# Gated cross-attention with a routed feed-forward: where ScalarE rounds the expert weights, and in which order GpSimd serves roots and low parts

## The chip, the cores and the metric

The kernel runs on one core of one Trainium2 chip. The metric is the device time of one execution in microseconds (us), lower is better; the median of three runs is compared.

## The reference

Eight batches of 256 rows of 512 numbers. First an attention over a context, added to the rows with a gate; then a layer normalisation, a router that picks two of eight experts for each row, and the two experts' feed-forward, again added with a gate. All is float32.

```python
x = x + tanh(g_xattn[0]) * xattn(layernorm(x), ctx_2048, mask)
x = x + tanh(g_ffn[0]) * ffn(layernorm(x), w_router, w_gate, w_up, w_down)
# xattn: softmax(mask(h @ ctx.T / sqrt(512))) @ ctx
# ffn: probs = softmax(h @ w_router.T); top 2, rescaled to sum 1
#      sum over the two experts of p * (silu(h @ Wg.T) * (h @ Wu.T)) @ Wd.T
```

## The kernel before

It has two stages. The first, some 125 us long, walks over 16 tiles of 128 rows (NTK = 16, two tiles to a batch): attention, second normalisation, router, and a table that sorts the rows by expert. The second gathers the sorted rows and runs the experts over 36 to 39 tiles. The change touches the first stage only.

The first stage is a software pipeline written out by hand. Each of the five engines runs its own program, a loop `for s in range(STEPS)`, and works in step s on several tiles at once, each at another place of its way. Semaphores join the programs; within one engine the order is as written, so an instruction that waits holds back all that stand behind it.

What matters of a step s:

- TensorE (PE): `t1(s)` transposes the normalised tile (L914), `tp(s-2)` transposes the softmax numerators (L920), `score(s-1)` (L932), the router product `rt(s-4)` (L962), the attention product `pv(s-2)` (L943), `t2(s-3)` transposes the second normalised tile (L951), and in odd steps the small products `cum` and `tab` of the sorting table (L974 to L986). From step 16 on `pv` stands ahead of `rt`.
- ScalarE (ACT): copies out of PSUM `ev2(s-4)` (L486) and `ev1(s)` (L463), the first normalisation `xln(s+1)` (L493), two stores, `evp(s-2)` (L479), in odd steps a small exponential (L524), then the second normalisation `x2ln(s-3)` (L501), the softmax exponential `exp(s-1)` (L470), and last the roundings `hi(u)` (L506) of the step's weight blocks.
- VectorE (DVE): a main list, with one operation of a side list woven in after each of its operations. Main: `X` update of tile s-3 (L652), its statistics (L611, L614, L617), the statistics of tile s+2 (the same lines), the bias `nb2(s-3)` (L626), the row maximum (L632), the bias `nb1(s+2)` (L626 again), the reciprocal (L644). Side: router top 2 and sorting, such as `dd` (L672), `MS` (L681), `Qi` (L703), `rr` (L706), `TA` (L711), four `TB` (L718), and `cc`, `pc`, `comb` (L730 to L737). In even steps the side list runs from the top 2 to two of the `TB`; in odd steps from the other two to `comb`.
- GpSimd (POOL): the two roots of a step, `rstd` of tile s-3 (`rs2`) and of tile s+2 (`rs1`), both at L370, and the low parts `lo(u)` at L379.

The expert weights come in 40 blocks of 128x512. ScalarE writes the rounded value of a block (`hi`, which signals `s_wh`), and GpSimd then writes the difference between the block and its rounding (`lo`, which waits for that signal). `units(s)` names the blocks of a step: one in steps 1 and 2, two in steps 3 to 17, one in steps 18 to 21; the other four are done in the second stage. SyncE loads the blocks of step s+2 during its own step s.

VectorE has to have `rs2` for `nb2`, and `x2ln(s-3)` needs `nb2`; PE's `t2(s-3)`, the last large product of its step, needs `x2ln(s-3)`.

Of the kernel before, what the change touches and what calls it, by code (L numbers as in the profile page):

```python
# [8 lines left out]
NTK = 16  # L9
# [12 lines left out]
NXT = 7  # L22
EPS = 1e-5
RB = 6
AHEAD = 12

SCALE = float(D) ** -0.5
# [2 lines left out]
def flamingo(nc, x, ctxn, ctxt, mask, gates, wr, wgu, wd1, wd2, cst, cstb, out):  # L30
# [11 lines left out]
    with ctx:  # L42
# [209 lines left out]
        def part(u):  # L252

            return u // 5, (u % 5 if u < NU - 5 else (u - 1) % 5)

        def wunit(u):

            e, n = part(u)
            if n < 3:
                c = slice(1536 * e + 512 * n, 1536 * e + 512 * n + 512)  # L260
                return wgu[3 * e + n], WGlf[:, c].bitcast(fp32), WGhf[:, c], WGlf[:, c]
            if n == 4:
                return wd2[e], WS[:, e % 2, :], WD2[:, e, :], WD2[64:128, e, :]
            return wd1[e], WD1l[:, e, :].bitcast(fp32), WD1h[:, e, :], WD1l[:, e, :]

        def units(s):

            return range(*[min(NUA, sum(SPLIT[:max(0, n)])) for n in (s, s + 1)])
# [6 lines left out]
        def tiles_of(eng):  # L275

            eng.wait_ge(s_ln, 1)
            return eng.value_load(LN[0:1, 0:1], min_val=NF, max_val=NT)

        def lives(eng, n, j):  # L280

            return eng.If(n > j) if j >= NF else nullcontext()
# [73 lines left out]
        @block.gpsimd  # L356
        def _(pool):
            pool.wait_ge(s_c, 16)

            last = [None]  # L360

            def settle():

                if last[0]:
                    pool.wait_ge(*last[0])

            def rstd(mv, k, rs, s_in, s_out):
                last[0] = (s_out, k + 1)
                pool.wait_ge(s_in, k + 1)
                pool.tensor_tensor(out=rs[:, k:k + 1], in0=mv[:, k, 1:2], in1=mhalf, op=ALU.pow).then_inc(s_out, 1)  # L370

            def lo(u):
                pool.wait_ge(s_wh, u + 1)
                _, raw, hi, low = wunit(u)
                half = part(u)[1] == 4
                p = slice(64, 128) if half else slice(0, 128)
                if half:
                    settle()
                pool.tensor_tensor(out=low, in0=raw[p], in1=hi[p].bitcast(fp32), op=ALU.subtract).then_inc(s_wl, 1)  # L379
                last[0] = (s_wl, u + 1)  # L380
                if half:
                    settle()

            rstd(mv1, 0, rs1, s_st1, s_rs1)
            rstd(mv1, 1, rs1, s_st1, s_rs1)
            for s in range(STEPS):
                if s != NTK + 2:
                    for u in units(s - 1)[0:1]:
                        lo(u)
                if 0 <= s - 3 < NTK:  # L390
                    rstd(mv2, s - 3, rs2, s_st2, s_rs2)
                for u in units(s - 1)[0 if s == NTK + 2 else 1:]:
                    lo(u)
                if s + 2 < NTK:
                    rstd(mv1, s + 2, rs1, s_st1, s_rs1)


            pool.wait_ge(s_ixg, 1)
            pool.wait_ge(s_sy[0], 16 * 8)
            pool.wait_ge(s_sy[1], 16 * 8)  # L400
            pool.wait_ge(s_scb, 16 * 8)
            for i in range(4):
                pool.wait_ge(s_so[i], 16 * 4)

            def gather(j):
                if j >= NX:
                    pool.wait_ge(s_tx, j - NX + 1)
                    pool.wait_ge(s_cj, j - NX + 1)
                pool.indirect_dma_start(out=XG[:, j % NX, :], out_offset=None, in_=x2s,  # L409
                                        in_offset=bass.IndirectOffsetOnAxis(ap=IXG[:, j:j + 1], axis=0))\  # L410
                    .then_inc(s_g[j % NX], 16)

            def landed(n):

                for i in range(NB):
                    if (n + NB - 1 - i) // NB:
                        pool.wait_ge(s_add[i], 16 * ((n + NB - 1 - i) // NB))

            def fence(j):

                with pool.If((turns[(j - 1) // 13] & (1 << (j - 1) % 13)) != 0):
                    landed(j)

            for j in range(NX):
                gather(j)
            pool.wait_ge(s_tn, 1)
            pool.wait_ge(s_ixi, 1)
            turns = [pool.value_load(TN[0:1, g:g + 1], min_val=0, max_val=(1 << 13) - 1) for g in range(3)]
            live = tiles_of(pool)
            for j in range(NT):  # L430
                with lives(pool, live, j):
                    pool.wait_ge(s_y, j + 1)
                    if j:
                        fence(j)
                    pool.indirect_dma_start(out=out, out_offset=bass.IndirectOffsetOnAxis(ap=IXI[:, j:j + 1], axis=0),  # L435
                                            in_=YT[:, j % NB, :], in_offset=None, compute_op=ALU.add)\
                        .then_inc(s_add[j % NB], 16)
                    if j + NX < NT:
                        gather(j + NX)
                    if j in HOLD:  # L440
                        lo(NUA + HOLD.index(j))
# [3 lines left out]
        def _(act):  # L445
# [36 lines left out]
            def ev2(k):  # L482
                act.wait_ge(s_t2, k + 1)
                if k >= 1:
                    act.wait_ge(s_rt, k)
                act.activation(Y2T[:, :, :], A1[:, :].rearrange("p (k c) -> p k c", k=KC), ACT.Copy)\  # L486
                    .then_inc(s_y2t, 1)
# [16 lines left out]
            def hi(u):  # L504
                act.wait_ge(s_ws[u % NST], 16 * (u // NST + 1))
                act.activation(wunit(u)[2], wunit(u)[1], ACT.Copy).then_inc(s_wh, 1)  # L506

            xln(0)
            for s in range(STEPS):
                if 0 <= s - 4 < NTK:  # L510
                    ev2(s - 4)
                if s < NTK:
                    ev1(s)
                if s + 1 < NTK:
                    xln(s + 1)
                stores(s)
                if 0 <= s - 2 < NTK:
                    evp(s - 2)
                if s >= 7 and s % 2 == 1 and (s - 7) // 2 < B:
                    b = (s - 7) // 2  # L520
                    act.wait_ge(s_dd, b + 1)
                    if b:
                        act.wait_ge(s_cb, b)
                    act.activation(e2[:, :, :], dd[:, :, :], ACT.Exp).then_inc(s_e2, 1)  # L524
                if 0 <= s - 3 < NTK:
                    x2ln(s - 3)
                if 0 <= s - 1 < NTK:
                    exp(s - 1)
                for u in units(s):
                    hi(u)  # L530

            act.activation(rsum[:, 0:1], rinv[:, 0:1], ACT.Silu)
            act.wait_ge(s_ejp, 1)
# [12 lines left out]
            def silu(j):  # L546
                act.wait_ge(s_gu, j + 1)
                if j >= 2:
                    act.wait_ge(s_h, j - 1)
                act.activation(SG[:, j % 2, :], SC[j % 2][:, 0:I], ACT.Silu).then_inc(s_sg, 1)  # L550
# [18 lines left out]
            for j in range(NT):  # L569
                with lives(act, live, j):  # L570
                    silu(j)
                    if j == AHEAD:
                        live = tiles_of(act)
# [13 lines left out]
        def _(dve):  # L587
# [87 lines left out]
            def ranks(b):  # L675
# [6 lines left out]
                yield  # L682
                if b >= RB:
                    return
# [205 lines left out]
            for j in range(NT):  # L890
                with lives(dve, live, j):
                    mul(j)
                    if j == AHEAD:
                        live = tiles_of(dve)
# [8 lines left out]
        def _(pe):  # L903
# [61 lines left out]
            def cum(b):  # L965
# [3 lines left out]
                else:  # L969
                    pe.wait_ge(s_gbc, 1)  # L970
                pe.wait_ge(s_rn, min(b, RB) + 1)
                for i in range(2):
                    o = PC[:, 8 * i:8 * i + 8]
                    pe.matmul(o, tri, MS[:, b, i, :], start=True, stop=False)  # L974
                    pe.matmul(o, onesb, ebr, start=False, stop=False)
                    for t in range(2 * RB, 2 * b) if b > RB else ():
                        pe.matmul(o, onesb, MS[:, t // 2, t % 2, :], start=False, stop=False)
                    if i:
                        pe.matmul(o, onesb, MS[:, b, 0, :], start=False, stop=False)
                    m = pe.matmul(o, onesb, Rn[:, min(b, RB), :], start=False, stop=True)  # L980
                m.then_inc(s_cum, 1)
# [11 lines left out]
            for s in range(STEPS):  # L993
# [32 lines left out]
                if s == 2 * B + 5:  # L1026
                    pe.wait_ge(s_ms, B)
                    pe.wait_ge(s_lc, B - 1)
                    for t in range(2 * RB, 2 * B):
                        pe.matmul(PL[:, 0:8], onesb, MS[:, t // 2, t % 2, :], start=(t == 2 * RB), stop=False)  # L1030
                    pe.matmul(PL[:, 0:8], onesb, Rn[:, RB, :], start=False, stop=True).then_inc(s_cnt, 1)
# [71 lines left out]
            for j in range(NT):  # L1103
                with lives(pe, live, j):
# [6 lines left out]
                    if j % 2 == 1 and 2 * j + 2 < NTP:  # L1111
                        own.update(experts(2 * j + 2))
                    if j == AHEAD + NT - NF:
                        live = tiles_of(pe)
# [69 lines left out]
```

## Time and profile before

| | |
|---|---|
| median of 3 runs | 290.98 us (290.82 to 292.32) |
| the profiled execution | 291.58 us, of it 289.8 us span |
| PE busy | 255.7 us, 88% of the span |
| DVE busy | 168.7 us, 58% |
| POOL busy | 164.1 us, 57% |
| ACT busy | 148.7 us, 51% |
| mean granted TensorE clock | 0.94 |

The profile is one execution of the program. A timeline row gives the start in us from the span's beginning, the duration, the engine, the line of the kernel, the operation with what it writes and reads, how many instructions the row merges, and in brackets how long the engine was idle before it and who released it. A duration that is longer than that of the same operation elsewhere holds time in which the instruction had begun and couldn't go on.

The first stage has three parts: the filling of the pipeline to about 40 us, the steady pairs of steps (an even and an odd one) to about 95 us, and the tail to about 126 us, where only the last tiles and the sorting table are left. The table is what the gathers of the second stage wait for.

### The profile page before, as it was taken

What the parts mean: (1) busy time and instruction counts of PE and PEld (TensorE: products, weight loads), DVE (VectorE), ACT (ScalarE), POOL (GpSimd) and SP (SyncE); (2) the same over time, 40 slices, a digit from 0 to 9 for tenths busy, and PEclk for the clock granted to TensorE, in tenths of its full rate; (3) what the DMA queues carried; (4) which work ended last, traced back from release to release, by engine and by line L of the source; (5) the groups of instructions that cost most, each with busy time, mean ns of one, the idle gap of its engine ahead of it and who ended that gap; (6) DMA issues with size and microseconds to landing.
All of it is one profiled execution on the core that took longest, in us unless ns stands there. A gap on an engine that the chain in (4) does not pass through costs nothing.

```text
span 289.8 us, 5422 instructions
## 1 busy us (share of the span) xinstructions
PE 255.7 (88%) x1501; PEld 217.7 (75%) x1501; DVE 168.7 (58%) x618; ACT 148.7 (51%) x310; POOL 164.1 (57%) x151
## 2 busy tenths in 40 slices
PE   0999998999999974477999999999999999999940
PEld 0877876677877653366899999999899999999920
DVE  4466778999977899950444444544444554444420
ACT  3469865687775644300455554554454455444430
POOL 1246557556564529225066686884765838748470
PEclk9999999999999997555999999999999999999995
DMA  6995999897998238007058576775894966868584
GB/s 220 385 380 168 344 349 285 329 296 272 302 313 299 99 97 280 1 14 206 5 83 146 104 131 127 138 137 98 157 171 100 165 141 108 174 95 167 121 127 57
DMA packets 25950, 52.08 MB, mean 180 GB/s; under 512 B 5248, under 2 KB 5376, under 8 KB 25920
## 3 DMA queue, kind: packets, MB, share of 16 engines
q0 software_dynamic: 8304, 19.83, 37.6%
q1 hardware_dynamic: 13008, 23.50, 25.1%
q10 hardware_dynamic: 4608, 8.39, 7.6%
q8 instruction: 15, 0.25, 0.3%
q14 instruction: 15, 0.12, 0.1%
HBM read 33.81 MB, written 17.89 MB: 178 GB/s over the span
## 4 chain that ended last, share of the span: by engine, by line
PE 62%; DVE 23%; issue 7%; ACT 3%; POOL 2%; DMA 1%; ACTq 0%; POOLq 0%; DVEq 0%
PE S L1070 9%; PE S L1071 9%; PE S L1074 9%; PE A L1060 6%; DVE st L611 4%; PE S L932 4%; PE PO L943 3%; DVE TB L718 3%; DVE X L652 3%; DVE TA L711 2%; PE PL L1093 2%; DVE dd L672 2%; PE A L914 1%; PE PO L1093 1%; PE PO L1095 1%
## 5 line engine op out<-in xcount | busy, mean ns | idle before, releaser
L435 POOL DMA_INDIRECT out<-YT,IXI x36 | 56.8, 1577 | 43.0 <-ACT YT L564 19.9
L1070 PE MATMUL S<-WGh,XTh 128*128 x144 | 52.4, 364 | 0.9 <-ACT XTh L543 0.9
L1071 PE MATMUL S<-WGl,XTh 128*128 x144 | 49.2, 342 | 0.0
L409 POOL DMA_INDIRECT XG<-x2s,IXG x39 | 38.5, 986 | 18.0 <-issue 9.1
L872 DVE TENSOR_TENSOR H<-SG,S 128x192 f32<-128x192 f32 x36 | 12.8, 354 | 48.3 <-ACT SG L550 40.7
L379 POOL TENSOR_TENSOR WGl<-WGl,WGh 128x512 fp32r<-128x512 f32 x24 | 30.5, 1275 | 14.5 <-ACT WGh L506 14.4
L550 ACT ACTIVATE SG<-S 128x192 f32<-128x192 f32 x36 | 11.9, 330 | 50.6 <-PE S L1074 49.1
L370 POOL TENSOR_TENSOR rs<-mv,CS 128x1 f32<-128x1 f32 x32 | 17.6, 551 | 30.8 <-DVE mv L617 30.8
L865 DVE TENSOR_TENSOR XTl<-A,XTh 128x512 fp32r<-128x512 f32 x37 | 25.6, 692 | 14.1 <-ACT XTh L543 13.1
L943 PE MATMUL PO<-CX,PT 128*128 128x512 f32 x64 | 31.2, 610 | 1.8 <-ACT PT L479 1.8
L1074 PE MATMUL S<-WGh,XTl 128*128 x144 | 31.5, 342 | 0.0
L932 PE MATMUL S<-CT,XLT 128*128 128x256 f32 x128 | 31.2, 388 | 0.0
L1070 PEld LDWEIGHTS S<-WGh,XTh 128*128 128x128 f32 x144 | 27.6, 192 | 1.7 <-issue 1.6
L1071 PEld LDWEIGHTS S<-WGl,XTh 128*128 128x128 f32 x144 | 27.8, 193 | 0.0
L543 ACT ACTIVATE XTh<-A 128x512 fp32r<-128x512 f32 x37 | 22.1, 598 | 9.5 <-issue 4.8
L932 PEld LDWEIGHTS S<-CT,XLT 128*128 128x128 f32 x128 | 23.9, 197 | 3.0
L1074 PEld LDWEIGHTS S<-WGh,XTl 128*128 128x128 f32 x144 | 26.1, 192 | 0.0
L611 DVE BATCH_NORM_STATS2 st<-X 128x6 f32<-128x512 f32 x32 | 22.0, 688 | 4.0 <-DMA X<-in_x 3.5
L1060 PE MATMUL A<-CS,XG 128*128 128x128 f32 x148 | 23.1, 281 | 1.1 <-DMA XG<-x2s,IXG 1.1
L501 ACT ACTIVATE Y<-X,nb,rs 128x512 f32<-128x512 f32 x16 | 13.0, 813 | 21.1 <-DVE nb L626 20.9
L1060 PEld LDWEIGHTS A<-CS,XG 128*128 128x128 f32 x148 | 19.0, 145 | 2.9 <-issue 1.4
L943 PEld LDWEIGHTS PO<-CX,PT 128*128 128x128 f32 x64 | 11.0, 191 | 10.0 <-issue 7.7
(151 smaller groups left out, 534.3 us busy)
## 6 DMA issues: line engine op xcount, KB each, us to landing
WGl<-in_wgu SPq DMA_DIRECT2D x24, 256.0 KB, 6.2
X<-in_x SPq DMA_DIRECT2D x16, 256.0 KB, 5.2
CT<-in_ctxt SPq DMA_DIRECT2D x8, 512.0 KB, 6.4
CX<-in_ctxn SPq DMA_DIRECT2D x8, 512.0 KB, 5.5
out<-X ACTq DMA_DIRECT2D x16, 256.0 KB, 5.8
x2s<-Y ACTq DMA_DIRECT2D x16, 256.0 KB, 5.1
WD1l<-in_wd SPq DMA_DIRECT2D x8, 256.0 KB, 5.3
WS<-in_wd SPq DMA_DIRECT2D x8, 256.0 KB, 4.6
```

Source lines behind the costliest of these rows:

```text
L379: pool.tensor_tensor(out=low, in0=raw[p], in1=hi[p].bitcast(fp32), op=ALU.subtract).then_inc(s_wl, 1)
L409: pool.indirect_dma_start(out=XG[:, j % NX, :], out_offset=None, in_=x2s, in_offset=bass.IndirectOffsetOnAxis(ap=IXG[:, j:j + 1], axis=0))\
L435: pool.indirect_dma_start(out=out, out_offset=bass.IndirectOffsetOnAxis(ap=IXI[:, j:j + 1], axis=0), in_=YT[:, j % NB, :], in_offset=None, ...
L543: act.activation(XTh[:, j % 2, :, :], (A0, A1)[j % 2][:, :].rearrange("p (k c) -> p k c", k=KC), ACT.Copy).then_inc(s_xh, 1)
L611: n = mark(dve.bn_stats(st[:, k % 2, :], src))
L865: dve.tensor_tensor(XTl[:, j % 2, :, :], (A0, A1)[j % 2][:, :].rearrange("p (k c) -> p k c", k=KC), XTh[:, j % 2, :, :].bitcast(fp32), ALU ...
L932: m = pe.matmul(SC[k % 2][:, 0:S], XLT[:, k % 2, c, :], CT[:, b % 2, c, :], start=False, stop=(c == KC - 1))
L943: m = pe.matmul(PO[:, :], PT[:, k % 2, c, :], CX[:, b % 2, c, :], start=(c == 0), stop=(c == 1))
L1060: m = pe.transpose((A0, A1)[j % 2][:, 128 * c:128 * c + 128], XG[:, j % NX, 128 * c:128 * c + 128], ident)
L1070: pe.matmul(o, XTh[:, j % 2, c, :], WGh[:, bass.ds(e, 1), c, :], start=(c == 0), stop=False)
L1071: pe.matmul(o, XTh[:, j % 2, c, :], WGl[:, bass.ds(e, 1), c, :], start=False, stop=False)
L1074: m = pe.matmul(o, XTl[:, j % 2, c, :], WGh[:, bass.ds(e, 1), c, :], start=False, stop=(c == KC - 1))
```

## The change

From step LATE = 5 on, ScalarE does the roundings of the step ahead of `x2ln(s-3)` and `exp(s-1)`, not behind them. GpSimd in a step did one low part of the step before, the root of tile s-3, the other low part of the step before, the root of tile s+2. It now does the root of tile s-3, the first low part of the same step, the root of tile s+2, the second low part of the same step. Step 5 does four low parts, those of step 4 ahead of all. The exception for step 18 goes away. Nothing is added to what is computed or moved.

```diff
+LATE = 5
@@ GpSimd
             for s in range(STEPS):
-                if s != NTK + 2:
-                    for u in units(s - 1)[0:1]:
+                if s <= LATE:
+                    for u in units(s - 1):
                         lo(u)
                 if 0 <= s - 3 < NTK:
                     rstd(mv2, s - 3, rs2, s_st2, s_rs2)
-                for u in units(s - 1)[0 if s == NTK + 2 else 1:]:
-                    lo(u)
+                if s >= LATE:
+                    for u in units(s)[0:1]:
+                        lo(u)
                 if s + 2 < NTK:
                     rstd(mv1, s + 2, rs1, s_st1, s_rs1)
+                if s >= LATE:
+                    for u in units(s)[1:]:
+                        lo(u)
@@ ScalarE
+                if s >= LATE:
+                    for u in units(s):
+                        hi(u)
                 if 0 <= s - 3 < NTK:
                     x2ln(s - 3)
                 if 0 <= s - 1 < NTK:
                     exp(s - 1)
-                for u in units(s):
-                    hi(u)
+                if s < LATE:
+                    for u in units(s):
+                        hi(u)
```

## Rows read from the trace of the kernel before

**Rows 1.** The page: each engine's busy time, share of the span, instructions.
```profile
PE 255.7 (88%) x1501; PEld 217.7 (75%) x1501; DVE 168.7 (58%) x618; ACT 148.7 (51%) x310; POOL 164.1 (57%) x151
```

**Rows 2.** Busy time in one stretch of 10 us, the first row naming the columns.
```profile
core 0: us, PE busy (x) PEld busy (x) DVE busy (x) ACT busy (x) POOL busy (x), PEclk, DMA share, GB/s
60.00:70.00 10.00, 10.00 (x54) 7.44 (x52) 9.90 (x43) 6.74 (x15) 6.44 (x8) 1.00 0.85 282
```

**Rows 3.** Timeline of PE over steps 10 and 11.
```profile
60.15 1.89 PE L932 MATMUL S<-CT,XLT 128*128 128x256 f32 x8
...
62.69 1.96 PE L943 MATMUL PO<-CX,PT 128*128 128x512 f32 x4
64.49 0.60 PE L951 MATMUL A<-CS,Y 128*128 128x128 f32 x4
...
68.23 1.96 PE L943 MATMUL PO<-CX,PT 128*128 128x512 f32 x4
70.24 0.66 PE L951 MATMUL A<-CS,Y 128*128 128x128 f32 x4
...
72.18 1.89 PE L932 MATMUL S<-CT,XLT 128*128 128x256 f32 x8
```

**Rows 4.** Timeline of DVE, ACT and POOL in the even step 10.
```profile
58.80 0.74 DVE L652 SCALAR_TENSOR_TENSOR X<-PO,rinv,X 128x512 f32<-128x512 f32 x1
...
60.82 0.55 POOL L370 TENSOR_TENSOR rs<-mv,CS 128x1 f32<-128x1 f32 x1 [0.33 <-DVE mv L617]
61.22 0.46 ACT L479 ACTIVATE PT<-S,GB 128x256 f32<-128x256 f32 x1
61.34 1.27 POOL L379 TENSOR_TENSOR WGl<-WGl,WGh 128x512 fp32r<-128x512 f32 x1
61.55 1.07 DVE L672 TENSOR_TENSOR dd<-mx 128x2 f32<-128x2 f32 x1
...
62.94 0.81 ACT L501 ACTIVATE Y<-X,nb,rs 128x512 f32<-128x512 f32 x1 [1.25 <-DVE nb L626]
63.25 0.16 DVE L703 TENSOR_SCALAR Qi<-sl 128x4 int32<-128x4 f32 x1
...
63.64 0.68 DVE L711 TENSOR_TENSOR TA<-CS,Qi 128x512 fp32r<-128x512 f32 x1
...
64.11 1.14 ACT L506 ACTIVATE WGh<-WGl 128x512 fp32r<-128x512 f32 x2
64.80 1.28 POOL L379 TENSOR_TENSOR WGl<-WGl,WGh 128x512 fp32r<-128x512 f32 x1 [1.49 <-ACT WGh L506]
64.81 0.75 DVE L652 SCALAR_TENSOR_TENSOR X<-PO,rinv,X 128x512 f32<-128x512 f32 x1
```

**Rows 5.** The same in the odd step 11.
```profile
67.52 1.27 POOL L379 TENSOR_TENSOR WGl<-WGl,WGh 128x512 fp32r<-128x512 f32 x1
67.54 1.28 DVE L681 TENSOR_TENSOR MS<-OH 128x16 bf16<-128x16 f32 x1
...
69.84 0.16 DVE L730 TENSOR_TENSOR cc<-cc,e 128x2 f32<-128x2 f32 x1
...
70.67 0.17 DVE L644 RECIPROCAL rinv<-rsum 128x1 f32<-128x1 f32 x1 [0.44 <-ACT P L470]
...
70.82 0.75 DVE L652 SCALAR_TENSOR_TENSOR X<-PO,rinv,X 128x512 f32<-128x512 f32 x1
```

**Rows 6.** Timeline of the tail, steps 17 to 19, DVE, POOL and PE.
```profile
100.42 1.15 DVE L706 SCALAR_TENSOR_TENSOR rr<-Qi,sl 128x4 f32<-128x4 int32 x1
...
103.23 1.98 PE L943 MATMUL PO<-CX,PT 128*128 128x512 f32 x4 [1.77 <-ACT PT L479]
...
109.28 3.71 POOL L379 TENSOR_TENSOR WGl<-WGl,WGh 128x512 fp32r<-128x512 f32 x3
...
113.53 3.00 DVE L718 TENSOR_SCALAR TB<-CS,rr 128x128 fp32r<-128x128 f32 x4
...
116.90 0.19 PE L974 MATMUL PC<-MS,CB 128*128 128x8 bf16 x1 [3.22 <-DVE MS L681]
```

## The prediction

> **What bounds the kernel now.** I read the page first: PE is busy in 88% of the span, no other engine in more than 58% [rows 1]. An average over two stages says little about a change in the first, so I went on to the busy time by stretches. From 60 to 70 us PE is busy for the whole 10.00 us, at full granted clock, and DVE for 9.90 [rows 2]. So in the steady pairs of steps two engines are full at once. In the tail PE stands idle for 1.77 and for 3.22 us at a time, the second time for DVE's `MS` [rows 6]: the tail belongs to DVE.
>
> The timeline of PE gives the length of a pair, from one score product to that two steps on: 72.18 - 60.15 = 12.03 us. PE hardly waits in it. In the odd step the transposition `t2` begins at 70.24, 2.01 us after `pv` began at 68.23; back to back it is 1.80 (62.69 to 64.49 in the even step, where nothing is waited for), so some 0.2 us are lost [rows 3]. That is all that an earlier second normalisation can give back in a pair. ACT does wait there, 1.25 us in the even step for `nb2` [rows 4], and the change fills this gap with 1.14 us of roundings; but idle time of ACT is not what bounds a pair.
>
> Is DVE's 9.90 work? Look at the durations. `dd`, a subtraction of 2 elements for each row, takes 1.07 us, and `MS`, a sum of 16, takes 1.28. Each begins just behind the start of a low part of POOL (61.34 and 67.52) and ends with it (61.34 + 1.27 = 62.61, and 61.55 + 1.07 = 62.62) [rows 4, 5]. Small operations of that kind take some 0.15 to 0.18, as `Qi` and `cc` do in the same rows [rows 4, 5]. So such a DVE operation stands still while a low part runs. The `X` update, which begins at 64.81 beside the low part of 64.80, takes 0.75 as ever [rows 4]: it reads PSUM, and is not held. The place of a low part decides what it costs DVE.
>
> [...]
>
> **Part by part: the steady pairs.** Before, a pair has four low parts. Two run right behind `exp`, beside the `X` update and the statistics, which aren't held. Two follow the root `rs2` at once (60.82 and 61.34) and hold one side operation each [rows 4, 5]. Taking the held time out gives DVE's bare work. Even step: 64.81 - 58.80 = 6.01, less 1.07 - 0.15 = 0.92, is 5.09. Odd step: 70.82 - 64.81 = 6.01, less 1.28 - 0.17 = 1.11 and less 0.44 of waiting for `exp`, is 4.46. Together 9.55 [rows 4, 5]. DVE thus has 12.03 - 9.55 = 2.5 us of room in a pair, of which 2.03 are already used by held operations.
>
> After, the low parts are taken from ahead and put behind the roots. I walk DVE through both steps, times from the `X` update.
>
> Even step. `rs2` runs from 2.02. ACT ends `evp` at 61.22 + 0.46 - 58.80 = 2.9 today, and sooner against DVE once DVE falls behind PE; with half of the 1.14 for a rounding, and not ahead of 0.52 behind the root's start (2.5), low part one begins between 2.5 and 3.5 [rows 4]. I take 3.0, to 4.25. `dd` (2.75) now escapes. `Qi`, bare at 63.25 - 0.92 - 58.80 = 3.53, is held until 4.25: 0.7 us. The root `rs1` stands behind that low part on POOL; `nb1` waits for it, and DVE's whole queue stands behind `nb1`: `rs1` 4.25 to 4.80, `nb1` about 4.85, ahead of which it would stand at some 4.5 (`TA` bare at 63.64 - 0.92 - 58.80 = 3.92, `nb1` 0.1 ahead of it, and 0.7 for `Qi`), so 0.35 more. Low part two starts when the root leaves the engine, 0.52 after its start as at 60.82 and 61.34 [rows 4], at 4.77; `TA`, at 4.97, reads two SBUF operands (the constants and `Qi`) and is held until 6.04: 1.07. Step: 5.09 + 0.7 + 0.35 + 1.07 = 7.2 us, where it was 6.0.
>
> Odd step. The roundings are done when the root is. Low part one follows `rs2` as it does today and holds `MS` as today: 1.11. Then `rs1`, and low part two 0.52 behind its start; `cc` (L730), which comes 0.16 later, is held for 1.1. The wait for `exp` (0.44) goes, being covered. Step: 4.46 + 1.11 + 1.1 = 6.65, less about 0.1 of overlap at the end of held operations, 6.55.
>
> The pair: 7.2 + 6.55 = 13.75 us against 12.03. DVE is then the bound, and PE waits in the odd step: up to `nb2` that step is as today, so `t2` begins 70.24 - 64.81 = 5.43 behind its `X` update [rows 3, 4], and that comes later each pair. Steps 8 to 13 are such pairs (side list full, both roots there): 3 x 1.7 = +5.1 us.
>
> The bounds of that: if only one more operation is held in a pair (one of the two new ones falls where DVE waits anyway), DVE needs 9.55 + 3 x 1.0 = 12.6, +0.6 a pair, +1.8 in all. If all four hold for their full 1.27 and both roots come 0.35 late, 9.55 + 5.1 + 0.7 = 15.35, +3.3 a pair, +10. Nearest to the rows is about 1.1 for a held operation, which is what was measured twice; I take +5.1.
>
> **Steps 5 to 7, 14 and 15.** Up to step 7 the side list is short and DVE waits for PE, so the two moved low parts cost nothing: their cover is that wait, and without it they would cost as above. In step 14 and 15 `rs1` is gone and the two low parts stand back to back, 2.5 us long, across `dd`, `Qi`, two of the `TB` and then `MS`, which PE's `cum` waits for. Step 14 has room, since `pv` ends late; in step 15 I count one more held operation, +1.0 (0 to 1.3).
>
> **The tail.** Here the change pays. The low part that holds `rr` for 1.15 us ahead of the `X` update of step 17, and with it `evp` and `pv` (PE idle 1.77), is done a step sooner [rows 6]; it then holds `dd` a little: -0.5 (0 to -1.0). Three low parts run from 109.28 for 3.71 us, two more behind them, and DVE's chain to the table crawls: the four `TB` take 3.00 [rows 6]. After, two of the five are gone from there. But those of steps 19 and 20 still wait for roundings behind `ev2(15)`, and fall on the `TB`. The gain is at most 3.22, PE's wait for `MS`, behind which `rt(15)` is the next thing late [rows 6]; and at least 0. I take -0.9, the nearest to one held operation fewer.
>
> The loads of the blocks are issued a pair of steps (12.03 us) ahead of their use and the roundings move forward by 64.11 - 61.68 = 2.4 us [rows 4], so I cost that at nothing; had a load come late, `x2ln` would wait for it. ACT: 1.14 us of roundings fit its 1.25 us in the even step [rows 4], so `x2ln` starts no later than today.
>
> **Sum.** +5.1 + 1.0 - 0.5 - 0.9 = +4.7 us. On the profiled execution 291.58 + 4.7 = 296.3; that one lies 0.6 above the median of the runs, so against the median 290.98 + 4.7 = 295.7 us.
>
> **The rivals.** (1) Faster. The held operations fall into DVE's room and PE stays the bound. Then the 0.2 us of four odd steps, 0.5 at step 17 and 2.4 of the 3.22 in the tail are won: 290.98 - 0.8 - 0.5 - 2.4 = 287.3. For it speaks that DVE has 2.5 us of room; against it that 2.03 of these are used and that `TA` comes 0.2 us behind the start of a low part in any order of the rest. It decides at DVE's need for a pair: below 12.03 it is right. 17%. (2) No difference: one more held operation in a pair (+1.8 in all) against a tail of -1.9, 291 us, 13%. (3) Dearer: the full 1.27 each, +8.5 with a little back in the tail, 299.5, 8%. (4) My forecast, +2.5 to +7: 62%.
>
> **How the numbers follow.** Faster by over 0.5% (1.5 us, about what a measurement of this kernel can tell from no change): 0.17; within: 0.14; slower: 0.69. The range reaches from 290.2, which takes in the case of no difference, to 298.8. The likeliest case alone: 293.5 to 298.
>
> **What would show it.** The distance of two score products in steps 8 to 13: near 13.7, not 12.0. `TA` (L711) near 1.7 us and `cc` (L730) near 1.2 in most steps, `dd` back at 0.15. `nb` (L626) waiting for `rs`. `t2` waiting for `x2ln` by about 1.7 us in odd steps, though ACT waits less ahead of its roundings. In the tail `rr` at 0.15 in step 17, and the four `TB` of L718 at 113.53 under 3 us. I am wrong if DVE's `TA` is not held, or if PE's pair stays at 12.

## The result and the profile after

| | before | changed |
|---|---|---|
| median | 290.9 us (290.77 to 292.32, 4 runs) | 294.77 us (293.54 to 295.9, 4 runs) |
| ratio | | 1.0121, 95% interval 1.0085 to 1.0157 |
| the profiled execution | 291.58 us, span 289.8 | 293.54 us, span 291.7 |
| the same pair of kernels once more | 291.63 us (12 runs) | 294.01 us (5 runs), ratio 1.0083 (1.0048 to 1.0118) |

The changed kernel is slower by 2.4 to 3.9 us. The prediction was 295.7 us, +4.7, with a range of 290.2 to 298.8. The ratios, here and below, leave out runs that lie over 1.5% above the fastest of their kernel: three in all, of the kernels e8_gap6 and e9_before_gap4 of the last experiments.

The page of the changed kernel, busy time by engine. The columns are those of [rows 1].

```profile
span 291.7 us, 5422 instructions
PE 254.2 (87%) x1501; PEld 214.8 (74%) x1501; DVE 175.5 (60%) x618; ACT 150.0 (51%) x310; POOL 163.5 (56%) x151
```

The instruction counts are the same. DVE is "busy" for 6.8 us more (168.7 before) with no instruction added: that is time in which its operations stand still.

The timeline of the changed kernel in steps 10 and 11, DVE, ACT and POOL. Lines of DVE and PE are 9 higher than before, so L681 is `dd`, L712 `Qi`, L715 `rr`, L720 `TA`, L690 `MS`, L742 `pc`, L661 the `X` update.

```profile
60.15 0.74 DVE L661 SCALAR_TENSOR_TENSOR X<-PO,rinv,X 128x512 f32<-128x512 f32 x1
...
62.11 0.55 POOL L371 TENSOR_TENSOR rs<-mv,CS 128x1 f32<-128x1 f32 x1 [2.33 <-DVE mv L626]
62.33 1.14 ACT L511 ACTIVATE WGh<-WGl 128x512 fp32r<-128x512 f32 x2
...
62.90 0.13 DVE L681 TENSOR_TENSOR dd<-mx 128x2 f32<-128x2 f32 x1
...
63.03 1.27 POOL L380 TENSOR_TENSOR WGl<-WGl,WGh 128x512 fp32r<-128x512 f32 x1 [0.38 <-ACT WGh L511]
...
63.43 0.81 ACT L506 ACTIVATE Y<-X,nb,rs 128x512 f32<-128x512 f32 x1
63.74 0.59 DVE L712 TENSOR_SCALAR Qi<-sl 128x4 int32<-128x4 f32 x1
...
64.77 1.27 POOL L380 TENSOR_TENSOR WGl<-WGl,WGh 128x512 fp32r<-128x512 f32 x1
64.85 0.21 DVE L635 TENSOR_SCALAR nb<-mv,rs 128x1 f32<-128x1 f32 x1 [0.32 <-POOL rs L371]
64.98 1.62 DVE L720 TENSOR_TENSOR TA<-CS,Qi 128x512 fp32r<-128x512 f32 x1
...
67.09 0.74 DVE L661 SCALAR_TENSOR_TENSOR X<-PO,rinv,X 128x512 f32<-128x512 f32 x1
...
69.81 1.28 DVE L690 TENSOR_TENSOR MS<-OH 128x16 bf16<-128x16 f32 x1
...
72.14 1.27 POOL L380 TENSOR_TENSOR WD<-WS,WD 64x512 fp32r<-64x512 f32 x1
...
72.31 1.15 DVE L742 TENSOR_TENSOR pc<-OH,cc 128x32 f32<-128x32 f32 x1
...
73.58 0.75 DVE L661 SCALAR_TENSOR_TENSOR X<-PO,rinv,X 128x512 f32<-128x512 f32 x1
```

Compare [rows 4] and [rows 5]. `dd` is free (0.13, it was 1.07), but `Qi` takes 0.59, `nb` waits 0.32 for its root, and `TA` takes 1.62 where it took 0.68. In the odd step `MS` is held as before and `pc` is held besides. In the even step ACT does what it was moved for: the roundings fill the gap and `x2ln` starts with no wait (in the odd step it still waits for `nb2`, 1.70 us where it was 2.00). From one `X` update to that two steps on it is 73.58 - 60.15 = 13.43 us, where it was 12.02.

What PE makes of that, its timeline in step 11 and the step before it:

```profile
63.94 1.96 PE L952 MATMUL PO<-CX,PT 128*128 128x512 f32 x4
65.74 0.60 PE L960 MATMUL A<-CS,Y 128*128 128x128 f32 x4
...
69.48 1.96 PE L952 MATMUL PO<-CX,PT 128*128 128x512 f32 x4
72.50 0.66 PE L960 MATMUL A<-CS,Y 128*128 128x128 f32 x4 [1.06 <-ACT Y L506]
```

`t2` comes 3.02 us behind `pv` in the odd step, against 2.01 in [rows 3] and 1.80 with nothing to wait for.

The first stage's end, where the table of rows is written and the first gathered tile is transposed, in the kernel before and then in the changed one:

```profile
126.92 0.20 DVE L847 TENSOR_SCALAR IXG<-PC 128x40 int32<-128x40 f32 x1 [0.74 <-PE PC L1040]
...
131.70 1.09 PE L1060 MATMUL A<-CS,XG 128*128 128x128 f32 x4 [1.15 <-DMA XG<-x2s,IXG]
...
139.40 0.44 PE L1070 MATMUL S<-WGh,XTh 128*128 x1 [0.15 <-ACT XTh L543]
```
```profile
130.55 0.20 DVE L856 TENSOR_SCALAR IXG<-PC 128x40 int32<-128x40 f32 x1 [0.74 <-PE PC L1049]
...
135.37 0.63 PE L1069 MATMUL A<-CS,XG 128*128 128x128 f32 x4 [1.18 <-DMA XG<-x2s,IXG]
...
141.08 0.44 PE L1079 MATMUL S<-WGh,XTh 128*128 x1 [0.57 <-ACT XTh L552]
```

The table is 3.63 us later, the first transposition 3.67, but the product of the second tile only 1.68. In between lies the granted clock (PEclk, the third number from the end), by stretches, before and then changed:

```profile
130.00:135.00 5.00, 3.08 (x14) 2.45 (x12) 0.69 (x1) 0.60 (x1) 3.78 (x5) 0.50 0.73 201
135.00:140.00 5.00, 4.76 (x18) 4.02 (x18) 1.20 (x4) 1.31 (x3) 0.48 (x1) 0.60 0.37 114
```
```profile
130.00:135.00 5.00, 4.20 (x35) 3.81 (x35) 1.52 (x10) 0.53 (x1) 2.75 (x3) 0.55 0.22 59
135.00:140.00 5.00, 3.42 (x20) 2.95 (x20) 1.16 (x3) 0.93 (x2) 3.22 (x4) 1.00 0.72 204
```

Before, the first gathered tile is worked at 0.50 to 0.60 of full clock, and its transposition takes 1.09 us. In the changed kernel's profile the clock is back at 1.00 by then, and it takes 0.63. That gives back 2.0 us of the 3.67, and so the profiled execution ends only 1.96 us later. Why it is back sooner there was not tried, and the experiments below show that it does not go with the length of the first stage.

### The profile page after: what moved, and what is told of

Read it like the earlier page. It is cut to its first block, busy times and chain, and to the rows that moved or that the text cites. A ratio compares the mean times of both kernels' runs of the same rounds, so it can differ in the third digit from the quotient of the medians.

```text
span 291.7 us, 5422 instructions
## 1 busy us (share of the span) xinstructions
PE 254.2 (87%) x1501; PEld 214.8 (74%) x1501; DVE 175.5 (60%) x618; ACT 150.0 (51%) x310; POOL 163.5 (56%) x151
## 4 chain that ended last, share of the span: by engine, by line
PE 61%; DVE 19%; issue 5%; DMA 4%; ACT 3%; POOL 3%; SPq 2%; ACTq 1%; POOLq 0%; DVEq 0%
PE S L1079 9%; PE S L1080 9%; PE S L1083 9%; PE A L1069 6%; PE PO L952 4%; DVE TB L727 3%; DMA WGl<-in_wgu 3%; DVE st L620 3%; PE S L941 2%; DVE X L661 2%; DVE TA L720 2%; PE PL L1102 2%; POOL rs L371 2%; PE PO L1104 1%; PE PO L1102 1%
## 5 line engine op out<-in xcount | busy, mean ns | idle before, releaser
L1079 PE MATMUL S<-WGh,XTh 128*128 x144 | 51.6, 358 | 1.5 <-issue 0.9
L1080 PE MATMUL S<-WGl,XTh 128*128 x144 | 48.6, 337 | 0.0
L952 PE MATMUL PO<-CX,PT 128*128 128x512 f32 x64 | 32.8, 637 | 1.3 <-ACT PT L484 1.3
L1083 PE MATMUL S<-WGh,XTl 128*128 x144 | 30.9, 337 | 0.0
L1080 PEld LDWEIGHTS S<-WGl,XTh 128*128 128x128 f32 x144 | 27.2, 189 | 0.0
L1083 PEld LDWEIGHTS S<-WGh,XTl 128*128 128x128 f32 x144 | 25.5, 188 | 0.0
L1069 PE MATMUL A<-CS,XG 128*128 128x128 f32 x148 | 22.2, 272 | 1.2 <-DMA XG<-x2s,IXG 1.2
L1069 PEld LDWEIGHTS A<-CS,XG 128*128 128x128 f32 x148 | 18.4, 140 | 2.7 <-issue 1.4
L573 ACT ACTIVATE YT<-PL,cj 128x512 f32<-128x512 f32 x18 | 12.4, 690 | 11.2 <-PE PL L1107 10.1
```

Of the source, the lines that this page charges most:

```text
L952: m = pe.matmul(PO[:, :], PT[:, k % 2, c, :], CX[:, b % 2, c, :], start=(c == 0), stop=(c == 1))
L1069: m = pe.transpose((A0, A1)[j % 2][:, 128 * c:128 * c + 128], XG[:, j % NX, 128 * c:128 * c + 128], ident)
L1079: pe.matmul(o, XTh[:, j % 2, c, :], WGh[:, bass.ds(e, 1), c, :], start=(c == 0), stop=False)
L1080: pe.matmul(o, XTh[:, j % 2, c, :], WGl[:, bass.ds(e, 1), c, :], start=False, stop=False)
L1083: m = pe.matmul(o, XTl[:, j % 2, c, :], WGh[:, bass.ds(e, 1), c, :], start=False, stop=(c == KC - 1))
```

## Experiments

The theory: a low part on GpSimd holds side operations of VectorE such as `dd` (1.07 us for 0.13), `MS` (1.28 for 0.17) and `TA` (1.62 for 0.68) until it ends; the change moved more low parts onto them. The rivals: the roundings delay the normalisation on ScalarE; the root behind a low part is what costs; the low parts do not matter.

**ScalarE's part alone.**

```diff
 # from the changed kernel: GpSimd's loop is again
+                if s != NTK + 2:
+                    for u in units(s - 1)[0:1]:
+                        lo(u)
                 rstd(mv2, s - 3, ...)
+                for u in units(s - 1)[0 if s == NTK + 2 else 1:]:
+                    lo(u)
                 rstd(mv1, s + 2, ...)
```

> ScalarE's part of the change alone: from step 5 the roundings stand ahead of the second normalisation, GpSimd keeps the order of before (first low part of the step before, root of tile s-3, second low part, root of tile s+2). My theory (what costs is where the low parts fall on VectorE, not the roundings): about as before. The first low part has its rounding early now and can start right behind the root of tile s+2 of the step before, so it may fall on TA or on cc as in the changed kernel; then one of the two extra held operations is there and the time is +1 to +3 us. Rival (the roundings delay x2ln and exp on ScalarE): all of the +3.9 us is here, near 294.8, with TA and cc short. Pair of score products: 12.0 to 13.0 us by mine, 13.4 by the rival.

Measured 295.15 us against 291.64, ratio 1.0128 (1.0068 to 1.0188): all of the loss is there with ScalarE's part alone. I had expected one extra held operation and +1 to +3 us; it is two, and the rival had the time right. The rival also said that `TA` and `cc` would be short. `TA` is (0.68), but `rr` is held in its place and `cc` is held too. The pair is 13.50 us long (`X` updates at 60.23 and 73.73). Timeline of DVE, ACT and POOL in steps 10 and 11 of this kernel:

```profile
62.77 1.27 POOL L380 TENSOR_TENSOR WGl<-WGl,WGh 128x512 fp32r<-128x512 f32 x1
...
62.99 1.06 DVE L677 TENSOR_TENSOR dd<-mx 128x2 f32<-128x2 f32 x1
...
64.37 0.81 ACT L502 ACTIVATE Y<-X,nb,rs 128x512 f32<-128x512 f32 x1 [0.71 <-DVE nb L631]
...
64.71 1.27 POOL L380 TENSOR_TENSOR WGl<-WGl,WGh 128x512 fp32r<-128x512 f32 x1
...
64.88 1.13 DVE L711 SCALAR_TENSOR_TENSOR rr<-Qi,sl 128x4 f32<-128x4 int32 x1
...
66.05 0.68 DVE L716 TENSOR_TENSOR TA<-CS,Qi 128x512 fp32r<-128x512 f32 x1
...
72.24 1.14 DVE L735 TENSOR_TENSOR cc<-cc,e 128x2 f32<-128x2 f32 x1
```

With the rounding early, nothing keeps the first low part back any more, and it runs right behind the second root, onto `rr`. `x2ln` (L502) waits for DVE's `nb2` and not for the roundings, which speaks against the rival. But the time alone doesn't tell the two theories apart: early roundings and moved low parts came together. The next run parts them.

**Early roundings, low part kept back.**

```diff
 # from e1_act_only
                     for u in units(s - 1)[0:1]:
+                        if s > LATE and s - 1 <= NTK:
+                            pool.wait_ge(s_rc, s - 1)      # reciprocal of the step before, which now signals s_rc
+                            if s in (9, 11, 13):
+                                pool.wait_ge(s_oh, 4 * ((s - 9) // 2) + 2)   # its second TB
                         lo(u)
```

> ScalarE's roundings early as in e1_act_only, GpSimd's order of before, but the first low part of a step is kept back by a wait until VectorE has done the reciprocal of the step before (and in steps 9, 11, 13 the second TB), so that it runs beside the X update as in the kernel before. My theory (the late roundings were the cover: they kept that low part out of VectorE's side operations): the pair is back at 12.0 to 12.2 us and the time within 1 us of before, with dd and MS held as before and TA, rr, cc and pc free. Rival (roundings ahead of x2ln cost by themselves on ScalarE): the time stays near e1_act_only's, 3 to 4 us above before, the pair near 13.4.

Measured 293.4 us against 291.12, ratio 1.0072 (1.0046 to 1.0097). The time misses my bound of 1 us, the pairs do not. The `X` updates of steps 8 to 14 begin at 46.81, 52.77, 58.77, 64.80, 70.81, 76.94 and 82.95 us; in the kernel before at 46.84, 52.80, 58.80, 64.81, 70.82, 76.95 and 82.95. Step by step within 0.03 us of before, with the roundings ahead of `x2ln` all the while; timeline of ACT, DVE and POOL in step 10 of this kernel:

```profile
61.57 1.14 ACT L512 ACTIVATE WGh<-WGl 128x512 fp32r<-128x512 f32 x2
...
62.92 0.81 ACT L507 ACTIVATE Y<-X,nb,rs 128x512 f32<-128x512 f32 x1 [0.22 <-DVE nb L636]
...
63.63 0.68 DVE L721 TENSOR_TENSOR TA<-CS,Qi 128x512 fp32r<-128x512 f32 x1
...
64.80 0.74 DVE L662 SCALAR_TENSOR_TENSOR X<-PO,rinv,X 128x512 f32<-128x512 f32 x1
...
65.02 1.28 POOL L381 TENSOR_TENSOR WGl<-WGl,WGh 128x512 fp32r<-128x512 f32 x1 [1.72 <-DVE rinv L654]
```

The roundings cost nothing there, and the whole loss of the pairs is the place of the low parts. Of the 2.3 us, 1.6 come in steps 14 to 16, where my wait lets a low part go onto `Qi` (held 1.09 us) and `MS` (1.08 us), on which PE's `cum` waits: the score product of step 16 begins at 97.32, before at 95.71 (here and below counted from its first, small product).

**Short low parts, in the changed order and in the old one.**

```diff
-                pool.tensor_tensor(out=low, in0=raw[p], in1=hi[p].bitcast(fp32), op=ALU.subtract)
+                w = 8 if first <= u < NUA else 512
+                pool.tensor_tensor(out=low[:, 0:w], in0=raw[p][:, 0:w], in1=hi[p].bitcast(fp32)[:, 0:w],
+                                   op=ALU.subtract)
```

> The changed kernel, but the low parts of the blocks of steps 5 to 21 write only 8 of their 512 columns (the rest of the low part is left out); every wait, signal and order stays. My theory: with nothing to hold VectorE a pair of steps is back at TensorE's 12.0 us, and the held operations are back at 0.15 and TA at 0.68; the time falls below before, to 284 to 288 us, since the tail's held operations go too. Rival (the order of the waits, the root of tile s+2 behind a rounding, or the roundings ahead of x2ln): a pair stays near 13.4 and the time near 293.

> The kernel before with the same short low parts (8 of 512 columns for the blocks of steps 5 to 21). It gives what the low parts cost in the old order. My theory: the pairs stay at 12.0 us, TensorE's own; the tail wins 2 to 4 us (rr ahead of the X update of step 17, and Qi, rr, TB behind 109 us); 286 to 289 us. If the changed order is otherwise worth something, e2_small_lo is faster than this by 0.5 to 1 us (the 0.2 us of the odd steps, and the gap ahead of x2ln); if the two are equal, the order by itself is worth nothing and all of the +3.9 us is the place of the low parts. Rival (low parts do not matter): 291.

Changed order: 282.38 us (282.12 to 283.4), ratio to before 0.9697 (0.9643 to 0.9751). Old order: 283.05 us (282.32 to 283.29), 0.9706 (0.9651 to 0.976). With nothing to hold VectorE, no operation of the side list is over its bare time by more than 0.3 us in either, and the two orders lie 0.7 us apart, their ranges overlapping. The table comes at the same time in both, but in the changed order the clock is again full at the first transposition. The table and the first transposition in the old order, then in the changed one:

```profile
117.91 0.20 DVE L850 TENSOR_SCALAR IXG<-PC 128x40 int32<-128x40 f32 x1 [0.74 <-PE PC L1043]
...
122.65 1.08 PE L1063 MATMUL A<-CS,XG 128*128 128x128 f32 x4 [1.10 <-DMA XG<-x2s,IXG]
```
```profile
117.97 0.20 DVE L859 TENSOR_SCALAR IXG<-PC 128x40 int32<-128x40 f32 x1 [0.74 <-PE PC L1052]
...
122.78 0.63 PE L1072 MATMUL A<-CS,XG 128*128 128x128 f32 x4 [1.40 <-DMA XG<-x2s,IXG]
```

So neither the order of the waits nor the early roundings account for the loss; it needs the length of the low parts, and the price of the change is their place. Both times lie below my ranges: the low parts cost the kernel before 8.6 us, not 2 to 5. That is the price of their whole length, the roots that queue behind them included; DVE's busy time falls from 168.7 to 153.7 us. Nor was 12.0 us PE's own time for a pair: it is 11.76 in both (59.10 to 70.86 in the old order). In the old order the table is 9.0 ahead of before, though the score product of step 16 is only 1.7 ahead (93.97 for 95.71). The pairs have room; the tail has none, and there they cost 7.3 us.

**Both roots first.**

```diff
                 if 0 <= s - 3 < NTK:
                     rstd(mv2, s - 3, rs2, s_st2, s_rs2)
-                if s >= LATE:
-                    for u in units(s)[0:1]:
-                        lo(u)
                 if s + 2 < NTK:
                     rstd(mv1, s + 2, rs1, s_st1, s_rs1)
                 if s >= LATE:
-                    for u in units(s)[1:]:
+                    for u in units(s):
                         lo(u)
```

> The changed kernel with both roots of a step ahead of both low parts. It tells the wait of nb1 for the root behind a low part (0.35 us by my sum, 0.32 in the changed kernel's trace) from the held operations. My theory: that wait goes, Qi and MS escape, TB and cc are held instead, and the second low part follows at once and holds another one in the odd step: a pair of 12.5 to 13, the time +1 to +3 us against before. Rival (the root's wait is what costs): as before or faster.

Measured 292.61 us against 291.12, ratio 1.0058 (1.0028 to 1.0089), +1.5: inside what I wrote, and the rival, that the wait for the root is what costs, falls. The pair I had wrong: from the `X` update at 57.99 to that at 71.65 it is 13.66 us, not 12.5 to 13. Timeline of DVE in these steps (L712 `rr`, L717 `TA`, L736 `cc`, L743 `comb`):

```profile
61.78 1.12 DVE L712 SCALAR_TENSOR_TENSOR rr<-Qi,sl 128x4 f32<-128x4 int32 x1
62.95 1.71 DVE L717 TENSOR_TENSOR TA<-CS,Qi 128x512 fp32r<-128x512 f32 x1
...
69.07 1.23 DVE L736 TENSOR_TENSOR cc<-cc,e 128x2 f32<-128x2 f32 x1
70.34 0.18 DVE L739 TENSOR_TENSOR pc<-OH,cc 128x32 f32<-128x32 f32 x1
70.56 1.17 DVE L743 TENSOR_TENSOR comb<-pc 128x16 f32<-128x16 f32 x1
```

I had let `TA` win the race against the low part; it lost. Four held operations are in the pair again, one for each low part, and the pair is as long as in the changed kernel. The time is nonetheless 1 to 2 us below that of the changed kernel, and the table came at 128.44 us, 2.1 sooner. All of that is there by step 10, whose `X` update is at 57.99 for 60.15: `comb` is free in step 7 (0.17 for 1.11), and steps 8 and 9 have three held operations for four.

**The change in the tail only.**

```diff
-LATE = 5
+LATE = 16
 # GpSimd, up to step 16, in the order of before
+                if s <= LATE: lo(units(s - 1)[0:1])
                 rstd(mv2, s - 3, ...)
+                if s <= LATE: lo(units(s - 1)[1:])
                 # then as in the changed kernel
```

> The kernel before up to step 15, the changed order from step 16 on (step 16 does four or three low parts, those of step 15 too). My theory: the steady pairs are as before (12.0 us), and only the tail changes: two low parts fewer between 109 and 116 us, MS there 1 to 3 us sooner, the table for the gathers 1 to 3 us sooner. Time 288 to 290, if the TensorE clock comes back as it does in the kernel before. Rival (the tail's gain is not there, or is eaten by three low parts in a row in step 16): 291 or above.

Measured 290.55 us (288.62 to 292.0, 12 runs) against 291.64, ratio 0.996 (0.993 to 0.9989). A gain of 0.4%, less than I expected. The table came at 126.77 us in the profile, 0.15 sooner than before: the held operations in the tail have changed (`MS`, `Rt`, three `Qi`, `pc`, `cc`) and hardly become fewer. But this profile is of the slowest of the 12 runs, and its clock fell to 0.50 by 102.5 us, in the kernel before only behind 110; so it can't size the tail's gain. The changed kernel itself gives back 1.1 us there, from the score product of step 16 to the table, in both of its profiles.

**The low parts of the tail on VectorE, behind the table.** The kernel before has VectorE idle for 4.89 us between the table and the first gathered tile. These kernels leave nothing out. In the table below, the kernel before took 291.12 us beside the first two and 291.63 beside the third.

```diff
+GAP = 5 * 8 - 4 - 4        # blocks 32 to 35, of steps 18 to 21; 30 to 35 in the second
             def lo(u):
+                if GAP <= u < NUA:
+                    return
@@ VectorE, behind the last operation of the table
+            for u in range(GAP, NUA):
+                dve.wait_ge(s_wh, u + 1)
+                dve.wait_ge(s_wl, u)
+                _, raw, hi, low = wunit(u)
+                p = slice(64, 128) if part(u)[1] == 4 else slice(0, 128)
+                dve.tensor_tensor(out=low, in0=raw[p], in1=hi[p].bitcast(fp32), op=ALU.subtract).then_inc(s_wl, 1)
```

> e4_tail_only (the order of before to step 15, the changed one from step 16) with the low parts of steps 18 to 21 (four blocks) taken from GpSimd and done by VectorE once the sorting table is out, where it is idle for some 5 us ahead of the first expert tile. My theory: four low parts fewer to hold VectorE in the tail; in e4_tail_only Qi, pc, Qi and cc lose 3.8 us to them. The table comes 2.5 to 4 us sooner; 4 x 0.6 us of VectorE work end ahead of the first tile's need. Time 286.5 to 289. Rival (the tail is bound by something else, such as the last router product): 290 to 291, as e4_tail_only.

> The same with the two blocks of step 17 too (six low parts, some 3.7 us on VectorE). My theory: about one more held operation goes (MS or Rt behind 104 us, 1 us), and VectorE's work now ends about when TensorE wants the weights, 0 to 0.5 us late: 0 to 1 us below e7_gap4. Rival: the gap is too short, and it is slower than e7_gap4 by 0.5 us or more.

> The kernel before with nothing of the change, but the low parts of steps 18 to 21 done by VectorE behind the table, as in e7_gap4. It parts e7_gap4's gain: what is the gap, what is the changed order in the tail. My theory: nearly all is the gap: 287.5 to 289, at most 1 us above e7_gap4, for the low parts of step 17 still run behind the last root and hold dd and Qi. Rival: the changed order in the tail is needed; 290 or more.

| kernel | median | ratio to before |
|---|---|---|
| e7_gap4, on the change in the tail only | 287.86 us (6 runs) | 0.9858 (0.9815 to 0.9901) |
| e8_gap6, the same with six blocks | 287.69 us (6 runs; 287.05 of the four counted) | 0.9859 (0.9816 to 0.9902) |
| e9_before_gap4, on the kernel before | 288.18 us (6 runs; 287.93 of the five counted) | 0.9846 (0.9801 to 0.9891) |

All three beat the kernel before and the changed one, and none can be told from the others. The changed order is not needed for it (e9 has none of it), and the two further blocks buy nothing that can be told. Timeline of e7_gap4, DVE and PE:

```profile
123.09 0.20 DVE L862 TENSOR_SCALAR IXG<-PC 128x40 int32<-128x40 f32 x1 [0.74 <-PE PC L1061]
...
124.87 0.69 DVE L881 TENSOR_TENSOR WGl<-WGl,WGh 128x512 fp32r<-128x512 f32 x1
...
125.66 0.69 DVE L881 TENSOR_TENSOR WD1l<-WD1l,WD1h 128x512 fp32r<-128x512 f32 x1
...
126.46 1.48 DVE L881 TENSOR_TENSOR WD<-WS,WD 64x512 fp32r<-64x512 f32 x2
...
128.04 1.09 PE L1081 MATMUL A<-CS,XG 128*128 128x128 f32 x4 [1.31 <-DVE WD L881]
```

The table is 3.83 us sooner than before, and PE's first tile 3.66: VectorE's four blocks end at about the time at which the gathered rows come. On VectorE a block takes 0.69 us (0.6 was the author's estimate); on GpSimd 1.27. With six blocks (e8_gap6) the gap is too short: the table is 5.9 sooner, at 121.01, but PE waits 2.90 us for VectorE and its first tile, at 127.56, is only 4.1 sooner.

The profile of e9_before_gap4 comes to the same end by another way:

```profile
125.88 0.20 DVE L850 TENSOR_SCALAR IXG<-PC 128x40 int32<-128x40 f32 x1 [0.74 <-PE PC L1049]
...
130.83 0.63 PE L1069 MATMUL A<-CS,XG 128*128 128x128 f32 x4 [1.31 <-DVE WD L869]
```

Its table is only 1.04 us sooner than before, but its clock is full at the first transposition, where that of e7_gap4 is half; the product of the second tile is then 3.61 sooner than before, in e7_gap4 3.66. So how much the gap alone brings the table forward isn't shown: these two profiles differ in the order and also in the clock, which in e9's fell to half by 105 us and in e7's only behind 110.

**The changed kernel once more.**

> The changed kernel once more, beside the kernel before on one chip. The granted clock at the start of the second stage was full in its first profile (first transposition of gathered rows 0.63 us) and half in the kernel before (1.09 us). My theory: the first stage is about 3.6 us longer in every run, and the end differs by up to 2 us with the moment at which the clock comes back; single times between +2 and +5 us against before, median about +3.5. Rival: the first result was chance and the median is within 1 us of before.

Measured 294.01 us (293.0 to 295.04, 5 runs) against 291.63, ratio 1.0083 (1.0048 to 1.0118), +2.4; the table at 131.54 us in its profile, 4.6 later than before, and the first transposition again 0.63 us, at full clock. So the late table is there a second time and so is the early clock. The single times lie 1.4 to 3.4 us above the median of before, a little below what I wrote. Only one run of each set is profiled, but each run has its mean granted clock on record. In the first set the two runs of the changed kernel at 0.950 and 0.953 took 293.95 and 293.54 us, the two at 0.940 and 0.941 took 295.9 and 295.6, some 4.7 to 5.0 above before; all five of this set are at 0.949 to 0.954. So the times of the changed kernel go with the clock, and half of the first set shows about the whole delay of the first stage (3.6 and 4.6 us in the profiles). A mean over the span does not say where the clock was low.

## Why the prediction was right

- **The bound and the held operations.** Right, and shown. DVE was full with PE, partly with operations that stood still, and one more for each moved low part made it the bound. The short low parts and the gate show it from both sides. Two reasons in the prediction were the author's estimates, and no run shows them: that the `X` update escapes because it reads PSUM, and that `TA` is held for its two SBUF operands (the term 1.07). The runs showed the `X` update at 0.75 us beside a low part, but also the statistics `st`, which read SBUF, at 0.69 beside one (0.67 to 0.70 else) in the kernel before; and in the changed kernel `TA` at 1.62 for 0.68, but also `Qi`, with one operand tensor, at 0.59 for 0.16.
- **The pair.** 13.43 us for the `X` updates where 13.75 were forecast; the score products of steps 8 to 14 took 40.45 us (47.27 to 87.72) against 36.51 (47.69 to 84.20), +3.9 instead of +5.1 (by the `X` updates of the same steps +4.4). A part of the difference is that the first of the three pairs was already 12.35 us long before, not 12.03. The rest are the holds: `Qi` cost 0.43 instead of 0.7 (the low part began 2.88 behind the `X` update for 3.0, `Qi` 3.59 for 3.53), `TA` 0.94 instead of 1.07, and in the odd step the second one 0.97 instead of 1.1. The root's wait was 0.32 for 0.35. That `pc` was held at one place and `cc` at another makes no difference.
- **Steps 14 and 15.** +1.2 us (12.70 against 11.51 from one score product to that two on), +1.0 forecast: in step 15 the `TB` stand for 1.8 us behind two low parts in a row, `MS` behind them, and PE's `cum` behind `MS`.
- **The tail.** From the score product of step 16, +4.7 us late, to the table, +3.6: 1.1 us given back, where 0.5 + 0.9 were forecast. But one part of the mechanism was not seen: the last `pv` took 3.51 us instead of 1.98, at a granted clock that had fallen by then (0.50 from 108 to 110 us, 0.72 over 105 to 110). What made it fall was not tried: PE had idled 1.27 us ahead of this product, but in the kernel before 1.77 us, and there the clock was 1.00 from 100 to 110. The `TB` were short of 3.00 as forecast, 2.06 us.
- **The sum for the first stage** was +4.7, measured +3.6 in one profile and +4.6 in the other. The second stage was taken as unchanged, and that step failed: by the product of the second tile it gave back 2.0 us in the first profile and 2.8 in the second (1.81 later, where the table was 4.62 later), with the clock full at the first transposition in both. Against before, +4.7 was forecast, and +3.9 and +2.4 were measured. So the way and the cause were right and the size was too high. That the first median comes so near (0.9 us) is in part luck: it hangs on its two runs with the lower mean clock, 295.6 and 295.9 us.
- **The rivals.** Faster would have needed a DVE pair below 12.03; it is 13.43. Roundings that delay `x2ln` were rightly cost at nothing. What I underrated is the room in the tail: I took the gain of moving low parts for at most 3.2 us, PE's wait for `MS`, but doing four of them elsewhere brings the table 3.8 us forward, and having none of weight brings 9.0.

## What to carry to other kernels

Before giving an engine an earlier start, look at what its late result was holding back on another: here a late rounding kept a GpSimd operation beside the VectorE work that doesn't mind it (the `X` update, 0.74 to 0.75 us beside it or not). Look for an operation of VectorE that is longer than its kin and ends with one of GpSimd: here `MS`, at 1.28 us for 0.17, was waiting, not working. Such time is to be counted as room that is used up. Work of GpSimd that only has to be done by a date is best put where VectorE is idle, even on VectorE itself; here that took the time down by 1.4 to 1.5%, more than any order of the same work that was tried. And two profiles whose clocks differ at some stage are to be compared ahead of that stage, not at their ends.

## What the runs showed of the hardware

- A GpSimd subtraction over 128x512 (1.27 us) held these VectorE operations until it ended: `dd`, bare 0.13, is shown as 1.07, `MS`, bare 0.15 to 0.18, as 1.28, and `TA`, bare 0.68, as 1.62 us. DVE is shown busy all the while (9.90 of the 10.00 us from 60 to 70 in the kernel before). The length of 30 such subtractions (the blocks of steps 5 to 21) costs the kernel before 8.6 us.
- The `X` update (0.74 to 0.75 us beside a low part or not), which reads one tensor from PSUM, was not held in the traces shown. Nor were, in the kernel before, the statistics `st` of 128x512 (0.69 us beside a low part, 0.67 to 0.70 else) and `nb` (0.21 beside one, 0.20 to 0.21 else). No run shows what parts these from the held ones.
- The same 128x512 subtraction took 0.69 us on VectorE and 1.27 on GpSimd.
- The granted clock at the start of the second stage can be at either level, with 2.0 us between the two in the pair of profiles above. It does not follow the length of the first stage: at the first transposition it was full (0.63 us) where the table came at 117.97, 125.88, 128.44, 130.55, 130.92 and 131.54 us, and half (1.08 or 1.09 us) where it came at 117.91, 121.01, 123.09, 126.77, 126.92 and 128.40. In three of the full ones (short low parts in the changed order, both roots first, ScalarE's part alone) it fell to 0.50 or 0.51 once more within 10 us. What decides it was not tried.
